# Quantised cross attention: the score bias moves to GpSimd, and the query transposes and pad copies lie later

## The reference

```python
def _L1_xattn_ref(x, cond, Wq, bq, Wkv, bkv, Wp, bp):
    q = (x @ Wq + bq).reshape(1, B * N, H, hd)
    kv = (cond @ Wkv + bkv).reshape(1, -1, 2, H, hd)
    k, v = (kv[:, :, 0], kv[:, :, 1])
    q = jnp.transpose(q * scale, (0, 2, 1, 3))
    ...
    q = _fq_sym(q, axis=-1)
    k = _fq_sym(k, axis=-1)
    v = _fq_sym(v, axis=2)
    attn = jnp.einsum('bhqd,bhkd->bhqk', q, k)
    attn = jax.nn.softmax(attn.astype(jnp.float32), axis=-1)
    attn = _fq_unsigned(attn, axis=-1)
    out = jnp.einsum('bhqk,bhkd->bhqd', attn, v)
    out = jnp.transpose(out, (0, 2, 1, 3)).reshape(B, N, C)
    return out @ Wp + bp
```

## Time and profile before

| | us |
|---|---|
| median of 3 runs | 637.98 (637.45 to 642.71) |
| the profiled execution | 638.7 |
| its span, first to last instruction | 637.0 |

### The profile page before, as it was taken

One profiled execution on the slowest core, in us unless ns is written; L12 is line 12 of the kernel. 1 busy time (PEld: TensorE's weight loads), 2 busy tenths in 40 slices (PEclk: granted clock), 3 DMA queues, 4 the chain that ended last, 5 costly groups with the idle time before them and its releaser, 6 DMA issues.

```text
span 637.0 us, 9905 instructions
## 1 busy us (share of the span) xinstructions
PE 405.7 (64%) x3391; PEld 266.5 (42%) x3424; DVE 448.6 (70%) x914; ACT 301.3 (47%) x540; POOL 285.1 (45%) x354
## 2 busy tenths in 40 slices
PE   2958653657888697577777777776653175556530
PEld 1526431435355565244444444443332164444420
DVE  6797999897819967898999998989963831111003
ACT  1452221443520166388787887878962023333320
POOL 6440829986272157111425324242010058888870
PEclk9987785795759999798998999989985569989985
DMA  8740000005100000199999999999993489885556
GB/s 295 205 172 1 0 1 2 0 1 99 35 0 2 0 4 5 39 179 160 180 165 171 184 169 182 164 171 177 183 177 120 137 267 220 203 188 87 87 69 206
DMA packets 187249, 74.89 MB, mean 118 GB/s; under 512 B 159232, under 2 KB 184768, under 8 KB 187200
## 3 DMA queue, kind: packets, MB, share of 16 engines
q1 hardware_dynamic: 181056, 65.35, 48.9%
q0 software_dynamic: 6144, 8.92, 7.9%
HBM read 27.56 MB, written 8.93 MB: 57 GB/s over the span
## 4 chain that ended last, share of the span: by engine, by line
DVE 49%; PE 23%; issue 11%; DMA 7%; POOL 6%; ACT 3%; POOLq 0%; SPq 0%; DVEq 0%; ACTq 0%
DVE nm L1386 21%; DMA A<-x_rows,slot_token 4%; DVE AT L1299 4%; PE ps L766 4%; PE ps L928 3%; POOL sums L597 2%; POOL A L583 2%; PE ps L989 2%; PE ps L1082 2%; PE ps L865 2%; DVE b L1392 1%; PE ps L785 1%; PE ps L940 1%; DMA sums<-A,slot_token 1%; DVE AT L1171 1%
## 5 line engine op out<-in xcount | busy, mean ns | idle before, releaser
L719 ACT ACTIVATE A<-ps,b,sq 128x1024 int16<-128x1024 f32 x128 | 154.2, 1205 | 41.4 <-DVE b L1392 36.7
L1386 DVE TENSOR_REDUCE nm<-ps 128x1 f32<-128x1024 f32 x128 | 154.9, 1210 | 8.8 <-PE ps L989 8.7
L989 PE MATMUL ps<-big,ctx_sb 128*128 128x512 bf16 x226 | 75.2, 405 | 53.2 <-ACT A L719 46.4
L1494 DVE TENSOR_TENSOR AT<-AT,ps 128x128 f32<-128x128 f32 x32 | 9.2, 288 | 85.6 <-ACT AT L736 85.6
L999 PEld LDWEIGHTS ps<-VI,A 128*128 128x128 f16 x1024 | 44.5, 98 | 42.0 <-DMA A<-A 13.4
L597 POOL DMA_INDIRECT sums<-A,slot_token x32 | 50.8, 1587 | 16.7 <-issue 8.5
L989 PEld LDWEIGHTS ps<-big,ctx_sb 128*128 128x128 bf16 x256 | 19.4, 102 | 75.0 <-ACT A L719 54.0
L999 PE MATMUL ps<-VI,A 128*128 128x16 f16 x1024 | 45.3, 171 | 7.9 <-DMA A<-A 7.7
L583 POOL DMA_INDIRECT A<-x_rows,slot_token x32 | 35.5, 1110 | 32.6 <-DVE slot_token L1484 23.1
L730 ACT ACTIVATE A<-ps 128x256 f32<-128x256 f32 x32 | 12.3, 384 | 61.6 <-PE ps L1072 61.2
L1072 PE MATMUL ps<-identf,A 128*128 128x128 f32 x64 | 15.0, 320 | 41.1 <-DMA A<-x_rows,slot_token 41.0
(11 more groups left out here) (280 smaller groups left out, 1008.9 us busy)
## 6 DMA issues: line engine op xcount, KB each, us to landing
A<-in SPq DMA_DIRECT2D x32, 256.0 KB, 3.4
A<-in SPq DMA_DIRECT2D x32, 128.0 KB, 3.7
A<-in SPq DMA_DIRECT2D x2, 1024.0 KB, 14.5
sums<-zeros SPq DMA_DIRECT2D x4, 512.0 KB, 5.1
A<-A SPq DMA_TRANSPOSE x128, 3.3
A<-sums SPq DMA_DIRECT2D x8, 256.0 KB, 4.5
X<-in SPq DMA_DIRECT2D x1, 1024.0 KB, 6.0
big<-in SPq DMA_DIRECT2D x1, 1024.0 KB, 8.6
```

What stands on the lines that cost most here:

```text
L719: a.activation(Y5[:, n % YB, :], ps[:, 2 * (n % 3):2 * (n % 3) + 2, :], ACT.Exp, scale=sq5[:, q, h:h + 1], bias=b5[:, n % 4:n % 4 + 1], ac ...
L989: done = T.matmul(ps[:, 2 * (n % 3) + c, :], QT5[:, q % 2, h // 2, h % 2, :], KT5[:, h // 2, c * 512:(c + 1) * 512], start=True, stop=True)
L1386: v.tensor_reduce(nm5[:, n % 4:n % 4 + 1], ps[:, 2 * (n % 3):2 * (n % 3) + 2, :].rearrange("p a c -> p (a c)"), AX.X, ALU.max, negate=True ...
```

## The change

The bias is taken from DVE's list and given to POOL's (score_bias). POOL now walks through the units as the other engines do: in each unit first the bias, then at most one side step, at a position of its own: the pad copies at positions 1 and 2 (one each), rstd and normalising of tile q + 2 at 5 and 6, of tile q - 1 at 7 and 8, the bias bp at 9, the query's rounding at 12, 13 and 14. SP issues the query's transpose behind the exponentials' transpose of position 0 of the next tile, where it stood behind position 14. DVE's maximum of unit n now waits until the bias of unit n - 4 has been made.

```diff
-                q = at_unit(n, 14)
-                if q is not None and q + 2 < NT:
-                    query_T(q + 2)
+                q = at_unit(n, 0)
+                if q is not None and 1 <= q < NT - 1:
+                    query_T(q + 1)
...
-            for q in range(NT + 1):
-                if 1 <= q < NT - 1:
-                    t = q + 1
-                    pool.wait_ge(S["q5T_loaded"], 16 * (t + 1))
-                    pool.wait_ge(S["s5_psum"], H * (t - 1))
-                    for e in range(2):
-                        g.tensor_copy(QT5[64 * e:64 * e + 64, t % 2, :, e, :], QR5[64 * e:64 * e + 64, t % 2, :, :]).then_inc(S["q5pad_ready"], 1)
-                    pool.wait_ge(S["q5pad_ready"], 2 * t + 2)
-                if q + 2 < NT:
+            def score_bias(n):
+
+                h, q = n % H, n // H
+                pool.wait_ge(S["max5_ready"], n + 1)
+                if n >= 4:
+                    pool.wait_ge(S["exp5_ready"], n - 3)
+                if h == 0 and q >= 2:
+                    pool.wait_ge(S["kq_step"], 8 * NT + 3 * (q - 2) + 1)
+                g.tensor_scalar(b5[:, n % 4:n % 4 + 1], nm5[:, n % 4:n % 4 + 1], sq5[:, q, h:h + 1], LN255, ALU.mult, ALU.add).then_inc(S["bias5_ready"], 1)
+
+            def pad_queries(n, t, e):
+
+                pool.wait_ge(S["bias5_ready"], n + 1)
+                pool.wait_ge(S["q5T_loaded"], 16 * (t + 1))
+                pool.wait_ge(S["s5_psum"], H * (t - 1))
+                g.tensor_copy(QT5[64 * e:64 * e + 64, t % 2, :, e, :], QR5[64 * e:64 * e + 64, t % 2, :, :]).then_inc(S["q5pad_ready"], 1)
+                pool.wait_ge(S["q5pad_ready"], 2 * t + e + 1)
+
+            for n in range(U5 + LAG5 + H):
+                if n < U5:
+                    score_bias(n)
+                q, at = (n - LAG5) // H, (n - LAG5) % H
+                if n < LAG5:
+                    continue
+                ahead = q + 2 < NT
+                scaled = ktmp[:, 0, :].rearrange("p (h d) -> p h d", d=HD)
+                if at in (1, 2) and 1 <= q < NT - 1:
+                    pad_queries(n, q + 1, at - 1)
+                if at == WO_H + 1 and ahead:
                     ln_rstd("q", q + 2, q + 3)
+                if at == WO_H + 2 and ahead:
                     ln_apply("q", q + 2)
+                if at == WP_H + 1 and q >= 1:
+                    ln_rstd("r", q - 1, q)
+                if at == WP_H + 2 and 1 <= q < NT:
+                    ln_apply("r", q - 1)
+                if at == WP_H + 3 and ahead:
                     add_bp(q + 2)
...
                     dve.wait_ge(S["s5_psum"], n + 1)
+                    if n >= 4:
+                        dve.wait_ge(S["bias5_ready"], n - 3)
                     v.tensor_reduce(nm5[:, n % 4:n % 4 + 1], ps[:, 2 * (n % 3):2 * (n % 3) + 2, :].rearrange("p a c -> p (a c)"), AX.X, ALU.max, negate=True).then_inc(S["max5_ready"], 1)
-                    dve.wait_ge(S["max5_ready"], n + 1)
-                    if n >= 4:
-                        dve.wait_ge(S["exp5_ready"], n - 3)
-                    if h == 0 and q >= 2:
-                        dve.wait_ge(S["kq_step"], 8 * NT + 3 * (q - 2) + 1)
-                    v.tensor_scalar(b5[:, n % 4:n % 4 + 1], nm5[:, n % 4:n % 4 + 1], sq5[:, q, h:h + 1], LN255, ALU.mult, ALU.add).then_inc(S["bias5_ready"], 1)
```

More of the change, by code:

```diff
@@ L559, in _ @@
                     ln_rstd("q", q + 2, q + 3)
+                if at == WO_H + 2 and ahead:
                     ln_apply("q", q + 2)
-                    add_bp(q + 2)
[L562 to L566, removed]
+                if at == WP_H + 1 and q >= 1:
+                    ln_rstd("r", q - 1, q)
+                if at == WP_H + 2 and 1 <= q < NT:
+                    ln_apply("r", q - 1)
@@ L567, in _ @@
+                if at == WP_H + 3 and ahead:
+                    add_bp(q + 2)
+                if at == Q5_H + 2 and ahead:
                     t = q + 2
-                    c = 8 * NT + 3 * q
                     pool.wait_ge(S["q5_step"], 5 + 3 * (q + 1))
                     g.tensor_scalar(sq5[:, t, :], sq5[:, t, :], 0.25, None, ALU.mult).then_inc(S["kq_step"], 1)
-                    heads = AT[:, t, :].rearrange("p (h d) -> p h d", d=HD)
-                    scaled = ktmp[:, 0, :].rearrange("p (h d) -> p h d", d=HD)
@@ L573, in _ @@
[L573 to L577, removed]
+                    g.tensor_tensor(scaled, AT[:, t, :].rearrange("p (h d) -> p h d", d=HD), rq5[:, t, :].unsqueeze(2).to_broadcast([P, H, HD]), ALU.mult).then_inc(S["kq_step"], 1)
@@ new lines, in _ @@
+                if at == Q5_H + 3 and ahead:
+                    pool.wait_ge(S["kq_step"], 8 * NT + 3 * q + 2)
+                    g.tensor_scalar(kpart[:, q + 2, :, 0, :], scaled, ROUND, -ROUND, ALU.add, ALU.add).then_inc(S["kq_step"], 1)
+                if at == Q5_H + 4 and ahead:
+                    pool.wait_ge(S["kq_step"], 8 * NT + 3 * q + 3)
+                    g.tensor_copy(kpart[:, q + 2, :, 1:3, :], kpart[:, q + 2, :, 0:1, :].to_broadcast([P, H, 2, HD])).then_inc(S["q5i_ready"], 1)
```

## The result

The changed kernel takes 655.84 us (median of 4 runs, 652.28 to 662.52), the kernel before on the same chip 637.80 us (4 runs, 637.45 to 642.71). The ratio is 1.026, with a 95% interval of 1.0205 to 1.0315: slower by 18 us. The forecast was 648.5, +10.5. The direction and the stall behind it were right, and the rise is 1.7 times the forecast. The time lies outside the forecast's own range (645 to 654) and inside the stated one (640 to 658), where rival C stood (656).

The account below looks back on a forecast made before the run. DVE was taken as the bound, 1.38 us a unit. First query transpose at 303.0, five periods of 28.7, then 6.15 + 32.2 put the last issue at 484.85 instead of 474.3: 638.0 + 10.5 = 648.5 us, range 640 to 658.

Parts of the forecast that it names:

- the stall: Biases on POOL queue behind its wait for the query transpose; the exponential two units on starts at Q + 4.85 us.
- rival C: PE's clock drops after idling in the stall, costing two units 0.7 each: 30.2 us a period, 656 in all; chance 0.15.
- DVE's share: Without the bias, DVE's time per unit in the changed stage falls from 1.38 to 1.12 us.
- The bias on POOL: POOL's 128x1 bias takes 0.25 us plus two handovers of 0.1, giving a round trip of 1.23 a unit.
- Q: Moment SP issues the query transpose, 1.37 us after that of m, the unit at position 0; m+2 is two units later.
- The first piece, up to Q1: Stage from its first transpose to the first query transpose, forecast at 303.0 us.
- The period: Time between successive query transposes: 4.85 + 1.30 + 17.2 + 3.9 + 0.05 + 1.37, in sum 28.7 us, up from 26.7.
- A: The forecast itself: 648.5 us, own range 645 to 654, a period 28.0 to 29.8; chance 0.50.
- The fourteen units and their side work: Within a period: 14 units at 1.23 us make 17.2, side work that sticks out adds 3.9.
- The last piece: From the sixth query transpose, 446.5, to the last issue, 484.85: 6.15 us, then 23 transposes and a store, 32.2.
- D: POOL's wait is no stall; the period falls to SP's 24.0 us, some -16 us, 622 in all; chance 0.13.
- B: The stall is there, but the rest runs at SP's issue pace: period 27.4 us, +4, 642 in all; chance 0.22.

Follow-up runs that it names:

- e7: The changed kernel run again unaltered, on another chip; 659.39 us, ratio 1.0359 to the kernel before.
- e5: Changed kernel with the query transpose back behind position 14 and the pad copies at positions 3 and 4; 631.12 us, ratio 0.9868 to the kernel before.
- e6: Changed kernel with the query transpose one unit later still, behind position 1; 665.90 us, ratio 1.0408 to the kernel before.
- e1: Changed kernel with the query transpose back behind position 14 of the tile before; 639.54 us, ratio 1.0061 to the kernel before.
- e8: Changed kernel with 38 unread products on PE at position 4 of tiles 1 to 6; 650.62 us, ratio 1.0211 to the kernel before.
- e5b: e5 run again on another chip; 626.59 us, ratio 0.9848 to the kernel before.
- e4: Kernel before with only the query transpose late, behind position 0 of the next tile, bias still on DVE; 637.20 us, ratio 0.998.
- e3: Changed kernel with the two pad copies at positions 3 and 4 instead of 1 and 2; 640.00 us, ratio 1.0026 to the kernel before.

## Why the forecast was right in kind and short in size

**DVE's share.** Right. Where scores are ready three maxima take 3.47 us (from 377.46 in the first execution), 1.125 apart; forecast 1.12. It is idle for 42 us.

**The bias on POOL.** Right: 0.266 in the mean against 0.25, and a handover of 0.10 from DVE. The handover to ACT is 0.03 (360.05 + 0.27 to 360.35), where 0.1 was taken. The Trainium skill, GPSIMD Engine Reference, section "Performance versus the Vector engine", gives a two-input add of 2048 columns on it about twice DVE's time; 0.266 to the 0.214 of the earlier trace rows is 1.25 times, so for one column the trace does not agree. Undisturbed exponentials start 1.18 to 1.20 apart, where I had 1.23: in such stretches ACT itself is the limit (380.98 and 382.16 in e7). But such stretches are short: half of all exponentials in e7 start 1.46 or more behind the one before.

**The stall.** Right to 0.05 us: the exponential of m+2 starts at Q + 4.80, forecast 4.85. The Trainium skill, DMA: Bandwidth & Descriptors, section "Rules for kernel authors", says to issue a DMA early and wait for it late; e5, where request and use were moved apart, and e6, where they were moved together, agree. e1 shows that "early" is counted from when the issuing queue gets there. Two signs of the stall were forecast too small. ACT waits 5.3, up to 5.9, not 4 to 5, and POOL's copies 34 us in six, not 18. The point Q itself lies later than I put it: ACT was free at Q - 0.5 and POOL at Q - 2.1 (358.93 - 5.47 = 353.46), because SP lags them.

**The first piece, up to Q1.** Right: 33.6 us from the first transpose (261.1 to 294.67), forecast 34.1 (268.9 to 303.0).

**The period.** This is the step that failed: 28.7 forecast, 30.42 measured. In the period from 355.55 (30.07 long) the exponential of m+16 ends at Q + 27.9 (forecast 27.25), and the next Q comes 2.2 behind it (forecast 1.42). Beside it lies a period of e8 at the full clock, from 357.66 (29.26 long), with 26.5 and 2.8. The two separate three terms:

- The low clock, left out of A and named in C at 1.5 a period. In e7 the exponential of m+7 starts 3.2 us after that of m+6, behind the 2.05 us projection; in e8 it is 2.2. With what the slower scores add, that of m+16 ends 1.4 later (27.9 against 26.5). SP's lag at the end, the next term, takes 0.6 of it back, so this period is 0.8 longer, and the mean of the five 1.0. I had given it a chance of 0.15 because the page showed one such dip in most periods already. That was the wrong question: PE idle for 4.2 us in every period is new, and a new dip follows it.
- "0.05 and the transpose of m+16, 1.37, up to the next Q". Measured 2.2 in e7 and 2.8 in e8. SP isn't free at the end of m+16's exponential: the last exponentials come 1.19 apart, faster than SP's 1.37, and now and then an issue takes up to 1 us more (below). 0.8 to 1.4 too small a period.
- The fourteen units and their side work, 17.2 + 3.9 = 21.1. Too large: in e8 they took 20.4. With 1.19 for an undisturbed unit instead of 1.23 the units take 0.56 less, which is most of the difference, and for side work 3.7 is left; the 3.9 was nearly right.

For the period from 355.55: 1.4 for the clock, 0.75 less for the units and 0.75 more for SP, together 1.4, which is 30.07 - 28.67. The mean of the five is 30.42; five times 1.7 above the forecast makes 8.6.

**The last piece.** 38.35 forecast, 40.6 measured (446.77 to 487.4). Of it 23 transposes and a store were to go at SP's pace. In e7 these start 1.47 apart in the mean instead of 1.37, 2.3 more. The term was the right one with a duration that left out the long issues.

The sum: 8.6 + 2.3 - 0.5 for the first piece = 10.4, and 215.95 (the stage forecast) + 10.4 = 226.3, the stage measured in e7. That execution is the fastest of its four; in the first one the stage is 228.2.

**The rivals.** D is excluded by e6 and by the stall in the timeline. B is wrong: its 27.4 assumed that SP sets the pace of the rest of the period, at 1.37; the period without the clock's share is 29.4. C was the case that came, with its price nearly right (1.5 forecast; 1.4 until the end of m+16's exponential, 1.0 to 1.2 in a period) and its end right (656) partly by luck: the lag of SP, which it lacks, made up the difference. Of the 10.4 us that the stage lies above its forecast about half is the clock. The rest is SP, its lag and its long issues, less what the units took less. That the time lies in the stated range is owed to C too, which had a chance of only 0.15 and carried the range up to 658.

**The slack of SP.** The prediction said that 2.7 us a period is the most that a lighter DVE can bring. With 1.45 for a transpose it is 26.66 - 25.3 = 1.4, and e5b got 1.2.

## What to carry to other kernels

When a small step of every unit moves to another engine, list everything that engine waits for: a wait that cost nothing in 63.8 us (e4) cost 3% as soon as the bias was queued behind it, and two units of distance at either end gave nearly all of it back (e1, e3), four gave a gain (e5). Count the distance between a request and its use in time, from when the issuing queue really gets to it; here SP reached the request when POOL was already one unit short of its use. And where a change makes an idle gap, price what the engine does after it as well: of some 20 us lost here 4 to 6 were PE's slow clock behind the gaps.

## What the runs showed of the chip that I had not expected

- A transpose issue of the same shape takes SP's queue 1.28 us in the median, but in every kernel 9 to 13 of the 128 take 1.6 to 2.8. Such an issue of the first execution, between two usual ones:

```profile
389.59 1.29 SPq L389 DMA_TRANSPOSE A<-A  x1
391.10 2.33 SPq L389 DMA_TRANSPOSE A<-A  x1
...
393.52 1.28 SPq L389 DMA_TRANSPOSE A<-A  x1
```

  In the kernel before they stand 13 to 18 us apart. From start to start, issues without a gap between them take 1.38 in the median and 1.44 to 1.45 in the mean (before, e5b). The cause was not looked for. A median hides it, and a sum of a hundred issues does not.
- PE's clock behind a gap: with 1.9 us of unread products in the gap the projection behind it took 2.05 us as without them, with 4.3 us of them 1.11 in five of six periods. Nothing between was tried.
- The 128x1 bias takes GpSimd 0.266 us and DVE 0.214, and ACT starts 0.03 us behind GpSimd's end: the engine is cheap for this; it was the queue in it that was dear.
